# Layer 0's owners loaded by fours and its shared expert in batches; layer 3's split with merged stores and its first heads filled on two queues

## The chip, the cores and the metric

The kernel runs on one core of a Trainium2 chip. The core has five engines with instruction streams of their own, which wait for each other on semaphores: TensorE (PE in the rows; PEld is its loading of weights, PEq its sequencer), VectorE (DVE), ScalarE (ACT), GpSimd (POOL) and SyncE (SP), which here only starts DMAs. GpSimd starts DMAs too, above all gathers and scatters by an index. The metric is the device time of one execution in microseconds; the time before is the median of three runs.

## What is computed

A decoder of four layers works on 2,048 tokens of 256 numbers (in this kernel 16 tiles of 128 tokens, or 4 groups of 512). Two of its parts are touched. The first is the feed-forward part of layer 0, a mixture of 32 experts of 128 inner columns, of which each token uses 8, and a shared expert that every token uses:

```python
def _L0_ffn_ref(hidden_states, Wr, br, Wg_s, bg_s, Wu_s, bu_s, Wd_s, bd_s, Wg, bg, Wu, bu, Wd, bd):
    aff = jax.nn.sigmoid(jnp.dot(x, Wr) + br)
    top_v, top_i = jax.lax.top_k(aff, K)                       # K = 8 of 32
    top_w = top_v / (jnp.sum(top_v, axis=-1, keepdims=True) + 1e-09)
    w_full = zeros.at[jnp.arange(T)[:, None], top_i].set(top_w)
    shared = jnp.dot(silu(jnp.dot(x, Wg_s) + bg_s) * (jnp.dot(x, Wu_s) + bu_s), Wd_s) + bd_s
    gate = silu(jnp.einsum('th,ehi->eti', x, Wg) + bg[:, None, :])
    up = jnp.einsum('th,ehi->eti', x, Wu) + bu[:, None, :]
    down = jnp.einsum('eti,eih->eth', gate * up, Wd) + bd[:, None, :]
    return shared + jnp.einsum('te,eth->th', w_full, down)
```

The second is the attention of layer 3, with 16 heads of 16 columns over all 2,048 tokens at once:

```python
def _L3_attn_ref(x, proj_w, proj_b, wq, wk):
    proj = jnp.einsum('bsd,ed->bse', x, proj_w) + proj_b
    flat = proj by heads: (H, B * S, hd)
    q = jnp.einsum('hnd,hde->hne', flat, wq)
    k = jnp.einsum('hnd,hde->hne', flat, wk)
    attn = jax.nn.softmax(jnp.einsum('hne,hme->hnm', q, k) / jnp.sqrt(D), axis=-1)
    out = jnp.einsum('hnm,hmd->hnd', attn, flat)
```

Both are called as `x = x + part(layernorm(x))`.

## The kernel before

**Layer 0's experts** (`l0_ffn`). Tokens are routed, and each token's row is scattered by GpSimd into tiles of 128 rows that belong to one expert each: 63 + 95 + 63 = 221 tile units. A table in memory, `owner`, holds the expert's number of each tile. TensorE's loop takes the units as a pipeline: in iteration u it transposes the tile of unit u+3 (`turn`, L2117), makes gate and up of unit u+2 (`up`: a bias product, L2127, and two products, L2133), the down product of unit u (`down`, L2149, behind a wait for VectorE's copy of the hidden rows), and the transposition of the hidden rows of unit u+1 (`turn_hidden`, a wait at L2139, the transposition at L2140). The weights of `up` and `down` are chosen by the expert's number, which must stand in a register of TensorE's sequencer. At the start of each 24th iteration a load (L2109) brings 24 of them. ScalarE copies the transposed tile and makes the silu; VectorE takes the result (`take`, L2340), copies the transposed hidden rows (L2349) and multiplies gate and up (L2355); in between it combines finished tokens at places that a table, COMBINED, fixes. SP reads tiles and writes results from a ring of four places.

Behind the tiles the same loop runs 16 more units for the shared expert, one for each tile of tokens: a bias product (L2130), two up products from the transposed tokens (L2133), the product with the chosen weights that brings the experts' down biases (L2147), the down product (L2149), the transposition (L2140), and an addition to x by VectorE (L2343). The tokens not yet combined are combined behind it.

**Layer 3's split** (`l3_attn`). For each of four groups of 512 tokens VectorE adds the gathered rows of layer 2's experts to x (L4567), takes mean and variance and normalises (L4549); TensorE transposes (L4508); ScalarE and VectorE copy one half each (L4594, L4554); TensorE projects (L4520) and makes queries and keys (L4530) by turns in two banks; ScalarE copies each with rounding to a shorter form (L4609, the first part) and VectorE subtracts that from it (L4561, the second part); SP stores both parts in device memory, eight stores of 256 KB a group (L4490). GpSimd gathers the rows (L4626) and then fills two lines of ones in each of four half tiles of keys (L4631).

**Layer 3's heads.** The heads go in eight pairs. For each pair SP loads three copies of 16 rows per head for queries and for keys from device memory (L4687), and two lines of zeros (L4689), 14 DMAs in all, the pairs by turns in two tiles. TensorE first makes the values (L4706), then probes (L4727), whose maxima VectorE takes (L4782), then scores and products with the values. The first probe waits for the 14 loads of pair 0.

The order on each engine is the order in which the code writes it; no planner stands in between. Instructions wait for semaphores alone.

Of the kernel before, what the change touches and what calls it, by code (L numbers as in the profile page):

```python
# [1847 lines left out]
def l0_ffn(k):  # L1848
# [16 lines left out]
    UNITS = BATCH + ALL  # L1865
    BATCHED = 24
# [3 lines left out]
    with ExitStack() as stack:  # L1870
# [3 lines left out]
        shared_bias = sb(k, stack, "shared_bias", [P, DIM])  # L1874
# [17 lines left out]
        affinity, rest = sb(k, stack, "affinity", [P, 8, E]), sb(k, stack, "rest", [P, 8, E])  # L1892
# [4 lines left out]
        mine, slots = sb(k, stack, "mine", [P, E * 8]), sb(k, stack, "slots", [P, E * 8])  # L1897
# [12 lines left out]
        tile_out = k.normed  # L1910
# [18 lines left out]
        def out_bank(u):  # L1929
            return k.ps[:, 5 + u % 2, 0:DIM]  # L1930

# [55 lines left out]
        with phase(k, "experts", names) as (block, s), ExitStack() as more:  # L1987
            for r in range(4):
                s[f"wrote{r}"] = more.enter_context(nc.semaphore(f"experts_wrote{r}"))
# [9 lines left out]
            def _(sp):  # L1999
# [6 lines left out]
                for m in range(ALL + 7):  # L2006
# [7 lines left out]
                    if m >= 7:  # L2014
                        j = m - 7
                        g = group_of(j)
                        sp.wait_ge(s["out_taken"], j + 1)
                        sp.dma_start(back_dram[g][sl(j - BEGIN[g]), :], tile_out[:, j % 4, :]).then_inc(s[f"wrote{j % 4}"], 16)
                for r in range(4):
                    sp.wait_ge(s[f"wrote{r}"], 16 * len(range(r, ALL, 4)))  # L2020

            @block.gpsimd
            def _(pool):
# [18 lines left out]
                for g in range(2):  # L2042
                    for r in range(4):
                        pool.wait_ge(s[f"wrote{r}"], 16 * len(range(r, BEGIN[g] + TILES[g], 4)))
# [9 lines left out]
            def _(pe):  # L2054
# [41 lines left out]
                def weight(u, at, width):  # L2096
                    if not is_tile(u):
                        return experts[:, E, at:at + width]
                    return experts[:, bass.ds(expert_of[u], 1), at:at + width].rearrange("p o d -> p (o d)")

                def turn(m):
                    if m == 0:
                        for job in (("choose", 2), ("own", 1)):
                            job_taken(pe, job)
                    if m % BATCHED == 0:
                        count = min(BATCHED, ALL - m)
                        if m <= BEGIN[2] < m + count:
                            job_taken(pe, ("own", 2))
                        _, values = nc.values_load_multi_w_load_instructions(  # L2109
                            owner[0:1, m:m + count], engines=[mybir.EngineType.PE], min_val=0, max_val=E - 1,  # L2110
                            skip_runtime_bounds_check_because="the owners are clamped to the last expert")
                        expert_of.update({m + j: value for j, value in enumerate(values)})
# [7 lines left out]
                def up(u):  # L2120
                    if u >= 2:
                        pe.wait_ge(s["multiplied"], u - 1)
                    t = u - ALL
                    if is_tile(u):
                        if u == 0:
                            pe.wait_ge(s["weighted"], 16 * 5)
                        nc.tensor.matmul(gate_bank(u), one_hot[:, u:u + 1].broadcast_to([3 * E, P]), bias_parts[:, :], start=True, stop=False)  # L2127
                        pe.wait_ge(s["tile_copied"], u + 1)
                    else:
                        nc.tensor.matmul(gate_bank(u), k.ident[:, 0:1].broadcast_to([P, P]), shared_bias[:, :], start=True, stop=False)  # L2130
                    for kt in range(KD):
                        x = tileT[:, u % 2, sl(kt)] if is_tile(u) else xT[t // GROUP][:, kt, sl(t % GROUP)]
                        last = nc.tensor.matmul(gate_bank(u), x, weight(u, 2 * kt * INNER, 2 * INNER), start=False, stop=kt == KD - 1)  # L2133
# [8 lines left out]
                def down(u):  # L2142
                    if u >= 2:
                        pe.wait_ge(s["out_taken"], u - 1)
                    if not is_tile(u):
                        t = u - ALL
# [3000 lines left out]
```

## Time and profile before

| | us |
|---|---|
| runs | 3310.62, 3321.85, 3310.62 |
| median | 3310.62 |
| the profiled execution's own time | 3318.16 |
| its span | 3315.8 |
| tile units of layer 0 (window) | 482 to 907 |
| additions of the shared expert | 909.2 to 941.5 |
| layer 3's split, first projection to first matmul of the heads | 2301.9 to 2362.3 |

Busy time over the whole span, from the page:

```profile
PE 2973.0 (90%) x20865; PEld 1843.2 (56%) x20865; DVE 2232.8 (67%) x4489; ACT 1809.1 (55%) x4182; POOL 1123.5 (34%) x1288
```

These shares are means over four layers with different limits, so the stretches that the diff touches have to be read one by one. Rows of the kinds below are read like this: a timeline row has its start, its length, engine, line, operation, output <- inputs and how many instructions it stands for, and in brackets how long the engine had been idle and what released it; a row by line has least, median and longest duration in ns. A matmul of 32-bit numbers stands as two records (two passes).

### The profile page before, as it was taken

To read this page: it belongs to the slowest core of one execution; us is meant where nothing else is said; L and a number is where in the kernel's file an instruction comes from. 1 tells how busy PE (TensorE), PEld (TensorE's weight loads), DVE (VectorE), ACT (ScalarE), POOL (GpSimd) and SP (SyncE) were. 2 spreads that over 40 slices of the span, in tenths; PEclk is the share of its full clock that TensorE was granted. 3 is DMA by queue.
4 is the path that set the end of the run, shared out by engine and by line. 5 is a ranking of instruction groups with operands and counts; after the bars stand their busy time and mean duration, and the time that the engine had idled before them with its cause. 6 is when DMAs were issued, how large, how long until landed. Compare 5 with 4: busy or idle time off the path is not lost. (4 is left out here: it accounts for less than half of the span.)

```text
span 3315.8 us, 59147 instructions
## 1 busy us (share of the span) xinstructions
PE 2973.0 (90%) x20865; PEld 1843.2 (56%) x20865; DVE 2232.8 (67%) x4489; ACT 1809.1 (55%) x4182; POOL 1123.5 (34%) x1288
## 2 busy tenths in 40 slices
PE   7979759999998799988799989787799999999989
PEld 4656548888755466643567757454333333333667
DVE  6777655455667566677577647424589999996772
ACT  6958723333333344445566645221278888888554
POOL 3535564442442022124266653012111112211333
PEclk9999859999999999999899999898889999999989
DMA  9400066666630000031000042132501111110400
GB/s 303 140 10 1 1 249 197 210 199 178 184 108 20 27 1 1 1 111 70 15 1 1 1 153 76 65 110 72 135 1 21 21 21 21 21 21 1 141 1 26
DMA packets 158226, 243.58 MB, mean 73 GB/s; under 512 B 21298, under 2 KB 130482, under 8 KB 152482
## 3 DMA queue, kind: packets, MB, share of 16 engines
q1 hardware_dynamic: 144114, 202.05, 19.9%
q0 software_dynamic: 13824, 37.77, 3.6%
q8 instruction: 172, 2.82, 0.4%
q14 instruction: 116, 0.95, 0.1%
HBM read 132.64 MB, written 107.10 MB: 72 GB/s over the span
## 5 line engine op out<-in xcount | busy, mean ns | idle before, releaser
L4782 DVE TENSOR_REDUCE peaks<-ps 128x2 f32<-128x1024 f32 x512 | 616.1, 1220 | 38.3 <-PE ps L4727 32.0
L4821 ACT ACTIVATE attn<-ps 128x512 f32<-128x512 f32 x1024 | 556.0, 596 | 97.3 <-PE ps L4717 38.5
L4727 PE MATMUL ps<-keys,queries 50*128 50x512 f32 x1024 | 375.2, 463 | 12.6 <-DVE peaks L4782 8.0
L4717 PE MATMUL ps<-queries,keys 50*128 50x512 f32 x1024 | 377.6, 454 | 0.0
L4741 PE MATMUL ps<-attn,head_values 128*32 128x256 f32 x4096 | 330.8, 395 | 2.5 <-ACT output L4832 0.4
L4717 PEld LDWEIGHTS ps<-queries,keys 50*128 50x128 f32 x1024 | 154.9, 188 | 206.5 <-ACT attn L4821 195.0
L1239 POOL TENSOR_TENSOR attn_w<-attn_w,attn_share 128x512 f32<-128x512 f32 x128 | 131.7, 1050 | 372.0 <-DVE attn_share L1085 372.0
L2133 PE MATMUL ps<-experts,tileT 128*128 x884 | 229.7, 382 | 0.0
L2340 DVE COPY normed<-ps 128x256 f32<-128x256 f32 x221 | 93.8, 424 | 183.5 <-PE ps L2149 181.7
L4741 PEld LDWEIGHTS ps<-attn,head_values 128*32 128x32 f32 x4096 | 82.2, 108 | 190.5 <-ACT attn L4821 171.5
L2194 ACT ACTIVATE tileT<-ps 128x256 f32<-128x256 f32 x221 | 84.8, 384 | 149.5 <-PE ps L2117 149.5
L4727 PEld LDWEIGHTS ps<-keys,queries 50*128 50x128 f32 x1024 | 149.8, 191 | 23.3 <-DVE peaks L4782 16.6
L2133 PEld LDWEIGHTS ps<-experts,tileT 128*128 128x128 f32 x884 | 151.8, 192 | 15.7 <-issue 0.5
L2200 ACT ACTIVATE gate<-ps 128x128 f32<-128x128 f32 x237 | 65.8, 278 | 163.7 <-PE ps L2133 163.7
L1076 DVE TENSOR_REDUCE attn_peak<-ps 128x4 f32<-128x512 f32 x128 | 87.6, 685 | 94.8 <-PE ps L958 94.8
L2149 PE MATMUL ps<-experts,hiddenT 128*128 (+1 forms) x474 | 144.9, 387 | 7.3 <-DVE hiddenT L2349 5.5
L4871 POOL CAST peak_parts<-peak 128x8 fp32r<-128x8 f32 x32 | 6.3, 198 | 393.9 <-DVE peak L4788 377.4
L2050 POOL DMA_INDIRECT rows<-expert_rows,index x96 | 91.5, 954 | 127.0 <-DMA expert_rows<-normed 60.8
L972 PE MATMUL ps<-xT,L_xattn_Wq 128*128 128x512 f32 x256 | 125.7, 614 | 7.7 <-ACT qT L1176 6.2
L2038 POOL DMA_INDIRECT routed_rows<-rows,index x96 | 95.6, 996 | 83.8 <-DVE normed L2340 58.4
L4886 POOL CAST queries<-peak_rows 2x128 fp32r<-2x128 f32 x256 | 73.5, 287 | 126.5 <-DVE peak_rows L4794 113.0
L2117 PE MATMUL ps<-ident,tile_in 128*128 128x128 f32 x442 | 85.6, 276 | 31.3 <-DMA tile_in<-routed_rows 20.4
(732 smaller groups left out, 7124.2 us busy)
## 6 DMA issues: line engine op xcount, KB each, us to landing
tile_in<-routed_rows SPq DMA_DIRECT2D x244, 128.0 KB, 2.3
expert_rows<-normed SPq DMA_DIRECT2D x221, 128.0 KB
routed_rows<-zeros SPq DMA_DIRECT2D x2, 8064.0 KB, 47.7
experts<-in_L_ffn_experts SPq DMA_DIRECT2D x4, 3072.0 KB, 21.0
routed_rows<-zeros SPq DMA_DIRECT2D x1, 12160.0 KB, 65.7
kT<-L_xattn_keys SPq DMA_DIRECT2D x8, 1024.0 KB, 4.8
v<-L_xattn_values SPq DMA_DIRECT2D x8, 1024.0 KB, 8.0
experts<-in_L_ffn_experts SPq DMA_DIRECT2D x8, 1024.0 KB
```

What stands on the lines that cost most here:

```text
L972: last = nc.tensor.matmul(query_bank, wq[:, kt, sl(4 * p + jj)], xT[g % 2][:, kt, :], start=kt == 0, stop=kt == KD - 1)
L1239: nc.gpsimd.tensor_tensor(w, w, share[:, n % 2, side, :].unsqueeze(2).broadcast_to([P, 4, P]), ALU.mult).then_inc(s_["scaled"], 1)
L2038: nc.gpsimd.indirect_dma_start(rows_dram[g][:, :], bass.IndirectOffsetOnAxis(index_of(slice(t, t + 1))[:, 0, c:c + 1], 0), rows[:, t, :], ...
L2050: nc.gpsimd.indirect_dma_start(rows[:, TOP * (t % 2) + c, :], None, back_dram[g][:, :], bass.IndirectOffsetOnAxis(index[:, t, c:c + 1], 0) ...
L2133: last = nc.tensor.matmul(gate_bank(u), x, weight(u, 2 * kt * INNER, 2 * INNER), start=False, stop=kt == KD - 1)
L2149: nc.tensor.matmul(out_bank(u), hiddenT[:, u % 2, :], weight(u, 2 * KD * INNER, DIM), start=is_tile(u), stop=True).then_inc(s["downed"], 1)
L2340: v.tensor_copy(tile_out[:, u % 4, :], out_bank(u)).then_inc(s["out_taken"], 1)
L4717: nc.tensor.matmul(bank(("score", n)), keys[pair % 2][rows, sl(kt)], queries[pair % 2][rows, sl(c, CHUNK)], start=True, stop=True).then_in ...
L4727: last = nc.tensor.matmul(k.ps[:, SB + p % PB, :], queries[pair % 2][rows, sl(t)], keys[pair % 2][rows, sl(c, CHUNK)], start=True, stop=True)
L4741: last = nc.tensor.matmul(mixed_bank[sl(strip, PAD), :], head_values[:, u // CHUNKS % 2, a, block, :], attn[:, (4 * m + 2 * half + a) % RI ...
L4782: v.tensor_reduce(peaks[:, r % 2, i // CHUNKS, :, i % CHUNKS], k.ps[:, at:at + 2, :], AX.X, ALU.max).then_inc(s["maxed"], 1)
L4821: nc.scalar.activation(attn[:, n % RING, :], bank(("score", n)), ACT.Exp, scale=1.0 / 16.0).then_inc(s["read"], 1)
```

## The change

It has two halves.

In layer 0, the owners are loaded by fours: `owners(m)` stands between the down product and the next hidden transposition, one iteration ahead of the unit that needs it. From unit 64 on, results go to eight places instead of four (the other four in a tile that is free by then), with eight semaphores. The shared expert leaves the loop: four batches of 512 tokens, with gate and up computed transposed (`shared_up`, four products of 512 columns), the biases as operands of the silu and of VectorE's product, so that neither a bias product nor a transposition is needed, then 16 down products with the product for the biases ahead of each; the first batch's up products are issued two units before the end of the tiles.

In layer 3's split, the two parts are stored by four stores of 512 KB a group; the first pair's queries and keys are copied from `parts` straight into their tiles, the queries by SP (six copies a group), the keys by GpSimd's queue (six a group), the lines of zeros by SP, the lines of ones by ScalarE. ScalarE makes both copies of the transposed tokens. Queries and keys have four banks. VectorE measures and normalises two groups ahead. The heads load from pair 1 on, and the first probe waits for no load.

The core of the diff (waits and names that follow from it are left out):

```diff
-    BATCHED = 24
+    LOADED = 4
+    WIDE = 64
...
+        def tile_out(u):
+            return outs[:, sl(u % 4, DIM)] if u >= WIDE and u % 8 >= 4 else k.normed[:, u % 4, :]
+
+        def out_before(u):
+            return u - 8 if u >= WIDE + 8 else u - 4 if u < WIDE + 4 else -1
...
+                def owners(m):
+                    count = min(LOADED, ALL - m)
+                    if m <= BEGIN[2] < m + count:
+                        job_taken(pe, ("own", 2))
+                    _, values = nc.values_load_multi_w_load_instructions(
+                        owner[0:1, m:m + count], engines=[mybir.EngineType.PE], min_val=0, max_val=E - 1,
+                        skip_runtime_bounds_check_because="the owners are clamped to the last expert")
+                    expert_of.update({m + j: value for j, value in enumerate(values)})
                 def turn(m):
-                    if m % BATCHED == 0:
-                        count = min(BATCHED, ALL - m)
...
+                def shared_up(i):
+                    if i == 1:
+                        pe.wait_ge(s["multiplied"], ALL)
+                    if i >= 2:
+                        pe.wait_ge(s["shared_multiplied"], i - 1)
+                    for half in range(2):
+                        for kt in range(KD):
+                            last = nc.tensor.matmul(shared_bank(i, half), experts[:, E, sl(2 * kt + half)], xT[i][:, kt, :], start=kt == 0, stop=kt == KD - 1)
+                    last.then_inc(s["shared_upped"], 1)
+
+                def shared_down(t):
+                    pe.wait_ge(s["out_taken"], ALL + t - 1)
+                    out = out_bank(ALL + t)
+                    nc.tensor.matmul(out, chosenT[t // GROUP][:, sl(t % GROUP)], bd[:, :], start=True, stop=False)
+                    pe.wait_ge(s["shared_multiplied"], t // GROUP + 1)
+                    nc.tensor.matmul(out, shared_hiddenT[t // GROUP % 2][:, sl(t % GROUP)], experts[:, E, 2 * KD * INNER:COLS],
+                                     start=False, stop=True).then_inc(s["downed"], 1)
...
+                    if u == ALL - 2:
+                        shared_up(0)
                     if u >= 0:
                         down(u)
-                    if 0 <= u + 1 < UNITS:
+                    if is_tile(u + 4) and (u + 4) % LOADED == 0:
+                        owners(u + 4)
+                    if is_tile(u + 1):
                         turn_hidden(u + 1)
+                for i in range(GROUPS):
+                    if i + 1 < GROUPS:
+                        shared_up(i + 1)
+                    for t in range(GROUP * i, GROUP * i + GROUP):
+                        shared_down(t)
...
+                def shared_silu(i):
...
+                    nc.scalar.activation(shared_gate[i % 2], shared_bank(i, 0), ACT.Silu, bias=shared_bias[:, 0:1]).then_inc(s["shared_silued"], 1)
...
+                def shared_multiply(i):
...
+                    v.scalar_tensor_tensor(shared_hiddenT[i % 2], shared_bank(i, 1), shared_bias[:, 1:2], shared_gate[i % 2],
+                                           ALU.add, ALU.mult).then_inc(s["shared_multiplied"], 1)
...
+                def first_pair(engine, g, side, part, done):
+                    dst, order = ((queries[0], Q_PARTS), (keys[0], K_PARTS))[side]
+                    for place in (at for at, kind in zip(PLACES, order) if kind == part):
+                        for a in range(2):
+                            to = TILE * a + place
+                            engine.dma_start(dst[to:to + D, sl(g, GT)].bitcast(F32), parts[g % 2][sl(a, D), part, side * KD, :].bitcast(F32)).then_inc(done, 16)
...
-                        for part, ready in enumerate((s["first"], s["second"])):
-                            for i in range(2 * KD):
-                                sp.wait_ge(ready, 2 * KD * g + i + 1)
...
+                        for side in range(2):
+                            for part, ready in enumerate((s["first"], s["second"])):
+                                sp.wait_ge(ready, 2 * KD * g + KD * side + 1)
+                                if side == 0:
+                                    first_pair(sp, g, side, part, s[f"stored{g % 2}"])
+                                sp.wait_ge(ready, 2 * KD * g + KD * side + KD)
+                                row0 = (side * 2 + part) * DIM
+                                sp.dma_start(parts_dram[row0:row0 + DIM, sl(g, GT)].rearrange("(m p) n -> p m n", p=P),
+                                             parts[g % 2][:, part, sl(side, KD), :].bitcast(F32)).then_inc(s[f"stored{g % 2}"], 16)
...
-                            nc.tensor.matmul(k.ps[:, 6 + i % 2, :], w[:, m, :], flat[g % 2][:, m, :], start=True, stop=True).then_inc(s["qk_made"], 1)
+                            nc.tensor.matmul(k.ps[:, 4 + i, :], w[:, m, :], flat[g % 2][:, m, :], start=True, stop=True).then_inc(s["qk_made"], 1)
...
+                    for g in range(2):
+                        measure(g)
+                        normalise(g)
                     for g in range(GROUPS):
...
+                        if g + 2 < GROUPS:
+                            measure(g + 2)
                         for i in range(2 * KD):
                             subtract(g, i)
+                        if g + 2 < GROUPS:
+                            normalise(g + 2)
...
-                    for i in range(2):
-                        for side in range(2):
-                            row0 = TILE * side + 2 * D
-                            nc.gpsimd.memset(keys[i][row0:row0 + 2, :].bitcast(F32), 1.0).then_inc(s["lined"], 1)
...
+                    for g in range(GROUPS):
+                        for part, ready in enumerate((s["first"], s["second"])):
+                            pool.wait_ge(ready, 2 * KD * g + KD + 1)
+                            first_pair(pool, g, 1, part, s[f"kept{g % 2}"])
...
-                for pair in range(PAIRS):
+                for pair in range(1, PAIRS):
...
-                        pe.wait_ge(loaded[pair % 2], 16 * 14 * (pair // 2 + 1))
+                        if pair:
+                            pe.wait_ge(loaded[pair % 2], loads_of(pair))
```

**TensorE, in a tile unit whose successor opens a new load.** First the order before (`owner` is the table of experts' numbers, L2149 the down product, L2140 the hidden transposition, L2117 the tile's transposition, L2127 the bias product):

```order
L2133 MATMUL ps<-experts,tileT 128x256
L2133 ISA
L2133 MATMUL ps<-experts,tileT 128x256
L2149 ISA
L2149 MATMUL ps<-experts,hiddenT 128x256
L2140 MATMUL ps<-ident,hidden 128x128
L2109 TENSOR_LOAD owner
L2117 MATMUL ps<-ident,tile_in 128x128 x2
L2127 MATMUL ps<-bias_parts,one_hot 128x256
```

The order of the changed kernel at such a place (its lines are L2157 down, L2121 load, L2151 hidden transposition, L2133 tile's transposition, L2141 bias, L2144 up):

```order
L2144 MATMUL ps<-experts,tileT 128x256
L2144 ISA
L2144 MATMUL ps<-experts,tileT 128x256
L2157 ISA
L2157 MATMUL ps<-experts,hiddenT 128x256
L2121 TENSOR_LOAD owner
L2151 MATMUL ps<-ident,hidden 128x128
L2133 MATMUL ps<-ident,tile_in 128x128 x2
L2141 MATMUL ps<-bias_parts,one_hot 128x256
```

The load moved ahead of the hidden transposition, and it stands in every fourth unit instead of every 24th.

**SP, storing two groups of layer 3's split.** Before, where L4490 is a store of one of the four tiles of a part, and L4687 the first load of the heads:

```order
L4484 DMA zero_rows<-zeros 16x256
L4490 DMA parts<-parts_332 128x512 x8
L4490 DMA parts<-parts_333 128x512 x8
L4490 DMA parts<-parts_332 128x512 x8
L4490 DMA parts<-parts_333 128x512 x8
```

In the changed kernel (L4545 a copy into the first pair's queries, L4569 a store of two tiles):

```order
L4557 DMA zero_rows<-zeros 16x256
L4560 DMA queries_321<-zero_rows 2x2048 x2
L4545 DMA queries_321<-parts_330 16x512 x4
L4569 DMA parts<-parts_330 128x2x512
L4545 DMA queries_321<-parts_330 16x512 x2
L4569 DMA parts<-parts_330 128x2x512 x3
L4545 DMA queries_321<-parts_331 16x512 x4
L4569 DMA parts<-parts_331 128x2x512
```

Eight stores of a group became four, with six copies of 16 rows among them.

**GpSimd, behind the sixteen gathers of the split.** Before, with the lines of ones of both tiles of keys:

```order
L4626 DMA expert_rows<-back_rows,place_back 128x256 x16
L4631 MEMSET keys_325 2x2048 x2
L4631 MEMSET keys_326 2x2048 x2
```

In the changed kernel, with the key copies of the first pair (`parts_330` and `parts_331` are the split's two turns):

```order
L4545 DMA keys_323<-parts_330 16x512 x6
L4545 DMA keys_323<-parts_331 16x512 x6
L4545 DMA keys_323<-parts_330 16x512 x6
L4545 DMA keys_323<-parts_331 16x512 x6
```

The fills are gone from this engine, and 24 copies stand there.

## Rows read from the trace of the kernel before

**Rows 1.** windows: busy us (and instructions) per engine, granted clock, DMA share, GB/s

```profile
482.00:907.00 425.00, 406.89 (x2268) 342.83 (x2269) 234.15 (x808) 152.25 (x451) 181.16 (x190) 0.99 0.64 196
844.00:847.00 3.00, 3.00 (x10) 2.35 (x9) 0.11 (x1) 0.66 (x2) 1.70 (x2) 0.50 0.53 163
2331.60:2344.60 13.00, 10.09 (x25) 3.87 (x24) 8.55 (x23) 4.58 (x9) 0.00 (x0) 0.89 0.44 161
2362.30:2377.80 15.50, 10.86 (x42) 8.90 (x42) 1.76 (x1) 2.99 (x5) 5.88 (x5) 0.83 0.99 134
2389.00:3030.00 641.00, 630.82 (x5875) 235.00 (x5877) 618.97 (x594) 542.71 (x1028) 119.52 (x407) 0.97 0.12 17
```

**Rows 2.** timeline of TensorE in the tile units: start us, length us, [idle before <- releaser]

```profile
574.60 0.27 PE L2140 MATMUL ps<-ident,hidden 128*128 128x128 f32 x1
574.71 0.38 PE L2117 MATMUL ps<-ident,tile_in 128*128 128x128 f32 x2
575.90 0.59 PE L2149 MATMUL ps<-experts,hiddenT 128*128 x2
576.34 0.27 PE L2140 MATMUL ps<-ident,hidden 128*128 128x128 f32 x1
577.97 0.30 PE L2117 MATMUL ps<-ident,tile_in 128*128 128x128 f32 x1 [1.36 <-issue]
```

**Rows 3.** loads of owners and one wait, by line: ns min/median/max, first and last start

```profile
L2109 PEldq TENSOR_LOAD <-owner x10: 841/1944/2040, 462.6 to 890.7; - x10
L2109 PEldq TENSOR_LOAD <-owner x1: 1987/1987/1987, 575.8 to 575.8; - x1
L2109 PEldq TENSOR_LOAD <-owner x1: 841/841/841, 890.7 to 890.7; - x1
L2139 PEldq EVENT_SEMAPHORE  x1: 51/51/51, 575.7 to 575.7; - x1
```

**Rows 4.** waits of TensorE, 482 to 907 us: total us, times, longest us

```profile
PE ps L2117 <- issue: 10.9, 9, 1.6
PE ps L2149 <- DVE hiddenT L2349: 5.2, 15, 0.8
```

**Rows 5.** shared expert's additions, by line

```profile
L2343 DVE TENSOR_TENSOR x<-ps,x x16: 424/425/425, 909.2 to 941.5; 128x256 f32<-128x256 f32 x16
```

**Rows 6.** timeline of the split

```profile
2301.85 5.17 PE L4520 MATMUL ps<-xT,L_attn_proj_w 128*128 128x512 f32 x8 [0.83 <-ACT xT L4594]
2307.94 7.47 POOL L4631 MEMSET keys<- 2x2048 f32 x4
2356.76 0.69 DVE L4561 TENSOR_TENSOR parts<-ps,parts 128x512 fp32r<-128x512 f32 x1 [0.35 <-ACT parts L4609]
```

**Rows 7.** by line: normalisations and gathers of the split, scattering gathers of layer 0

```profile
L4549 DVE TENSOR_SCALAR normed<-x,moments,rstd x16: 396/411/2024, 2298.5 to 2341.5; 128x256 f32<-128x256 f32 x16
L4626 POOL DMA_INDIRECT expert_rows<-back_rows,place_back x16: 946/946/1213, 2287.7 to 2307.0; - x16
...
  issue: 4.6, 15
...
L2038 POOL DMA_INDIRECT routed_rows<-rows,index x96: 956/960/2788, 435.0 to 599.6; - x96
```

**Rows 8.** stores of the split in the DMA view, median us to landing last

```profile
parts<-parts SPq DMA_DIRECT2D x32, 256.0 KB, 2.5
```

**Rows 9.** timeline where the heads begin

```profile
2362.30 10.85 PE L4706 MATMUL ps<-L_attn_proj_w,xT 128*128 128x256 f32 x40 [6.21 <-PEq L61]
2362.36 1.25 SPq L4687 DMA_DIRECT2D queries<-parts  x3
2377.79 1.22 PE L4727 MATMUL ps<-keys,queries 50*128 50x512 f32 x4 [4.64 <-DMA queries<-zero_rows]
2378.94 3.78 PE L4706 MATMUL ps<-L_attn_proj_w,xT 128*128 128x256 f32 x8
2383.64 1.99 PE L4706 MATMUL ps<-L_attn_proj_w,xT 128*128 128x256 f32 x8
```

More of the change, by code:

```diff
@@ L1987, in l0_ffn @@
         with phase(k, "experts", names) as (block, s), ExitStack() as more:
-            for r in range(4):
+            for m in ("shared_upped", "shared_silued", "shared_multiplied"):
+                s[m] = more.enter_context(nc.semaphore(f"experts_{m}"))
+            for r in range(8):
                 s[f"wrote{r}"] = more.enter_context(nc.semaphore(f"experts_wrote{r}"))
@@ L2042, in _ @@
                 for g in range(2):
-                    for r in range(4):
-                        pool.wait_ge(s[f"wrote{r}"], 16 * len(range(r, BEGIN[g] + TILES[g], 4)))
+                    for u in range(BEGIN[g + 1] - 8, BEGIN[g + 1]):
+                        written(pool, u)
                     for t in range(FIRST[g], FIRST[g] + SIZES[g]):
@@ L2096, in weight @@
                 def weight(u, at, width):
-                    if not is_tile(u):
-                        return experts[:, E, at:at + width]
                     return experts[:, bass.ds(expert_of[u], 1), at:at + width].rearrange("p o d -> p (o d)")
+                def owners(m):
[6 more added lines that the diff above has]
+                    expert_of.update({m + j: value for j, value in enumerate(values)})
                 def turn(m):
                     if m == 0:
-                        for job in (("choose", 2), ("own", 1)):
-                            job_taken(pe, job)
-                    if m % BATCHED == 0:
-                        count = min(BATCHED, ALL - m)
[L2107 to L2112, printed above, removed]
+                        job_taken(pe, ("choose", 2))
                     pe.wait_ge(s[f"read{m % 4}"], 16 * (m // 4 + 1))
@@ L2208, in _ @@
                 act.wait_ge(s["outered"], 1)
-                for u in range(-3, UNITS):
+                for u in range(-3, ALL):
                     for job in LATE:
@@ L2397, in _ @@
                         combine(t, c)
+                shared_multiply(0)
+                shared_multiply(1)
+                for i in range(GROUPS):
+                    for t in range(GROUP * i, GROUP * i + GROUP):
+                        shared_take(t)
+                    if i + 2 < GROUPS:
+                        shared_multiply(i + 2)
                 for t in LEFT:
@@ L4615, in _ @@
                         if g + 1 < GROUPS:
-                            root(g + 1)
                             take_x(g + 1)
```

160 lines of the change are left out of this document (89 added, 71 removed).

## The prediction

> **What bounds the kernel now.** I read the page's slices first, then windows over the places that the diff touches, then the timeline inside them. In the tile units of layer 0 TensorE is the bound: 406.9 of 425 us busy at granted clock 0.99, VectorE 234 [rows 1]. The same group shows the other stretches: in one group of layer 3's split TensorE is busy 10.1 of 13.0 us and VectorE 8.6, the DMA share 0.44, so a chain between engines sets the pace; at the start of the heads the DMA share is 0.99; and behind 2389 us TensorE and VectorE are both 97% busy. So a gain in the units counts only as TensorE time, a gain in the split counts as the end of the phase, which waits for its last store, and what the heads start earlier they keep to the end.
>
> **Part 1, owners.** One unit takes 1.74 us (two hidden transpositions, 574.60 to 576.34) [rows 2]. A load of 24 owners begins at 575.8 and takes 1.99 us; the next matmul starts at 577.97, about 0.17 after the load ends. Without it the matmul would follow the transposition by 0.11, as it did at 574.71 [rows 2, 3]. Over the stretch such gaps are 10.9 us in 9 [rows 4]; with the 0.16 by which each gap's last transposition is drawn out over its 0.11, 12.3 us. All of this goes: **-12.3**. After the load at 841.6 the clock was also at 0.50 for 3.0 us [rows 1], so 1.5 us of work were lost: **-1.5**.
>
> Added: 55 loads inside the loop, of four values (one of one). No load of four is in the trace. Ten loads run from 0.84 to 2.04, and the 0.84 is the one of five values [rows 3]; 24 values cost 1.99, so each further value costs (1.99-0.84)/19 = 0.06, and four cost 0.78. The new place is between a unit's down product and the next hidden transposition. There TensorE's sequencer is ahead: the wait in front of the transposition was passed at 575.7, and the transposition began at 576.34, 0.64 later [rows 2, 3]. A load costs what it is longer than that lead, plus the 0.17 behind it: 0.78+0.17-0.64 = 0.31, times 55 = 16.8. Some fall into units in which TensorE already waits for VectorE's combining (5.2 us in 15 waits [rows 4]; by the kernel's table of combining there are twelve such places of four units, so one load in each at about 0.15): -1.8. So **+15.0**. Behind a waiting load stand only the transposition and the next unit's matmuls; VectorE's copy of the hidden rows waits for them, and it is not the bound. Bounds: if values come at one price per four, (1.99-0.84)/4 = 0.29 per four, a load of four is 0.55 and costs 0.08, in all 4 to 5; if four cost as much as five (0.84), 0.37 each or 20; and if no lead survives, 0.95 each or 52.
>
> The Trainium skill, page "DMA: Bandwidth & Descriptors", section "Latency and other measured facts", says that a tensor_load has a floor of about 600 ns and that loads are unrolled by four to spread it. The shortest load here, 841 ns with five values, lies above that floor; by it four values cost 0.13 us each behind the lead, an estimate, and the sum of this part would be some 8 us lower.
>
> Part 1 with eight result places: no wait of VectorE for the writing of a result is in the list of waits, so the places cost and give nothing. Sum **+1.2**.
>
> **Part 2, shared expert.** In the before, each of 16 units costs TensorE a bias product, two up products, a bias-of-down product and a down product, each of 256 columns at 0.43 (575.90 to 576.34), and a transposition of 0.11 [rows 2]: 2.26 us, 36.2 in all; its adds span 32.3 us, and the last two units lack the up work [rows 5]. After it: four batches of four products of 512 columns, twice 0.43 each = 13.6; 16 times two products of 256 columns = 13.7; together 27.3. The silu and the product of one batch, 512 columns on ScalarE and VectorE, stand behind the up products of the next; where they are not covered by eight products of 256 columns they show as a stall, at most the pair of them, about 1.4 (two operations of about 0.69, as the VectorE subtraction of 512 columns [rows 6]); I take 0.6 three times. 29.1 against 36.2: **-7.1** (-9 with no stall, -4.5 with full ones). Layer 0 in all: **-5.9**, from -20 to +2 (the loads at 20, the stalls full).
>
> **Part 3, layer 3's split.** Before: the first projection starts at 2301.85 and runs partly at half clock, 5.17 us [rows 6]. Then POOL fills four lines of keys from 2307.94 on for 7.47 us [rows 6], and the four normalising operations of the second group, elsewhere 0.41 each, take up to 2.02 [rows 7]; the second transposition waits for them. That cost 7.70 instead of 1.4 us. From then on one group follows another by 13 us, since each of its four query and key products waits for a bank that VectorE frees. The last subtraction starts at 2356.76 [rows 6], a store lands 2.5 us after its issue [rows 8], and the next phase's first matmul is at 2362.30 [rows 9]. I put the end of the phase at 2361.8.
>
> After: the memset on POOL is gone, ScalarE writes the key lines; group 1 is normalised before group 0 is projected; the four products have four banks. Then TensorE alone sets the pace: per group 8 passes for the projection and 8 for queries and keys at 0.43, and 8 transpositions at 0.11: 7.7 us. The first projection starts 0.6 later, since ScalarE makes both copies: 2302.4 to 2307.4; queries and keys of group 0 end at 2311.7; the last group's at about 2334.5; the last subtraction 1.4 later.
>
> Two queues carry more. SP issues 10 DMAs a group instead of 8; at 0.42 (three in 1.25 [rows 9]) they take 4.2 of the 7.7, and the last store goes out near 2339 and has landed by 2341.5. POOL issues six key copies a group. No direct copy from POOL to a tile is in the trace; the nearest is the gather of 128 rows, sixteen of them at 0.95 and 0.31 between (4.6 us in 15) [rows 7], so six are 7.5 us. They start when a group's keys are split, so the last six are over at 2342.1; the last is issued at 2340.8 and lands, like a store, 2.5 later: 2343.3. That ends last: **-18.5**. Bounds: below by SP's price of an issue, with the end set by the last group's splitting, near 2339 and -22.8; above by the longest gather, 2.79 [rows 7], which is rival (d). Transfers: stores of 2 MB took 0.44 of 13.0 = 5.7 us of all 16 engines [rows 1]; a group's 12 copies of 16 rows, 0.39 MB, put up to 2.9 more into it, at the pace of the loads of the pair, 134 GB/s at share 0.99 [rows 1]: rival (b).
>
> The SP wait in front of the query copies holds back the stores behind it, and those only; POOL has nothing else in this phase but the 16 gathers, which are out before.
>
> **Part 4, start of the heads.** Before, the value products run from 2362.30 for 10.85 us, and the first probe starts at 2377.79 after 4.64 us of waiting for the first pair's loads [rows 9]: **-4.6**, since the pair is already there. Eight value products then took 3.78 at half clock, against 1.99 a little later [rows 9]; without the pause TensorE stays at its full clock: 1.8, and 0.4 on the probes: **-2.2** (nothing, if the 9 us of waiting at the end of the phase cost the clock instead). Layer 3 in all: -18.5-4.6-2.2 = **-25.3** (-20 to -30).
>
> **Sum.** -5.9-25.3 = -31.2 on the profiled execution's 3318.2 gives 3287.0. That execution lies 7.5 above the median of the runs shown, 3310.6, so the forecast is **3279.5**.
>
> **Rivals.** (a) Short loads at their floor: a load of four at 0.57 costs 0.10, 55 of them 5.5 instead of 16.8: 11 to 12 less, **3268**. For it: 0.84 for five values is one row, and nothing shows the slope between five and 24; against: the load of 0.84 was followed by a gap as long as its excess over its lead.
> (b) The split is bound by transfers: 5.7+2.9 = 8.6 a group from 2312 on, end 2346.5 instead of 2343.3: **3283**. For: share 0.99 where copies of 16 rows ran; against: only 0.44 for the stores.
> (c) The loads find no lead, since a stall of one unit leaves the sequencer without one at the next: 0.95 each, 52 instead of 16.8, less 2 or 3 in the waits that are there: **3312**. For: TensorE's queue runs dry at each load; against: the lead is set by VectorE's copy, and three units without a load lie between.
> (d) Slower: the POOL queue becomes the bound of the split. VectorE's operations that have both operands in the on-chip memory (combining, normalising) and POOL hold each other up: with the memset beside them, one normalisation took 2.02 instead of 0.41 [rows 7]. If each of the 24 copies takes 2.79+0.30 (the longest gather [rows 7]), they end at 2311.7+24*3.09 = 2385.9, landed at 2387.5, 25.7 later than before: +25.7-6.8-5.9 = +13, **3324**. It decides from 2.55 us a copy on, where the total is nought. Against: 96 gathers beside the tile units have a median of 0.96 [rows 7], the 16 in this phase run at 0.95 while VectorE combines [rows 7], and VectorE has some 3 us of such work in 7.7 (four combining and four normalising operations).
> The Trainium skill, page "SBUF — State Buffer", section "A bandwidth-pool intuition that's wrong (but worth ruling out)", states this rule: a DMA issued from GpSimd of about 620 ns alone takes about 3100 ns beside a VectorE copy, as its descriptors can't be written meanwhile. The sixteen gathers at 0.95, with VectorE's combining beside them, don't show it, so it keeps a small chance.
>
> **How the numbers follow.** Forecast 0.56 (its own range 3271 to 3290), (a) 0.14, (b) 0.15, (c) 0.08, (d) 0.07. A measurement can't tell less than about 0.5%, 16.5 us, from no change: faster means below 3294, slower above 3327. Forecast, (a) and (b) lie below 3294, less 0.07 for their upper tails: faster 0.78. (c), those tails and half of (d) lie between, 0.18; slower 0.04. Range **3262 to 3302**: (a) with the shared expert and the split at their better ends, up to (b) with the loads at 20 and the stalls full, and a part of (c).
>
> **What would show it.** The 57 owner loads: the short ones near 0.78, with gaps of about 0.15 to 0.3 before the hidden transposition; at 0.57 rival (a), and gaps near 0.9 rival (c). 16 shared adds at the end with no more than 29 us of TensorE's work. Normalisations of 1.4 us a group and a cadence of 7.7 in the split; POOL's copies at 0.95 and 0.3, or near 3 for (d); the heads' first matmul 18 us earlier, counted from the gathers; the first probe right behind the fifth pair of value products. The forecast is wrong if the split's cadence stays above 9, or if the tile units take longer than before by more than 5 us.

## The result, and the profile after

The changed kernel took 3258.9 us (median of 4 runs, 3256.3 to 3262.4) against 3310.6 before: ratio 0.985, interval 0.983 to 0.987. The forecast was 3279.5, with a range from 3262: right in sign, short by 21 us, and the time lies 3 us below the range. The profiled execution took 3259.7 us, its span 3257.9.

Where the time went can be read stage by stage, from the starts of a few instructions in the traces (second column of "changed": another execution of it, from the first experiment):

| stage, from and to | before | changed | forecast | measured |
|---|---|---|---|---|
| first to last result of the tile units | 418.2 | 404.9, 406.5 | +1.2 | -12 to -13 |
| from there to the end of the last shared addition | 35.0 | 25.8, 25.8 | -7.1 | -9.2 |
| split's first gather to the heads' first matmul | 74.6 | 60.5, 60.2 | -18.5 | -14.2 |
| from there to the ninth reduction of the heads | 28.8 | 21.4, 21.7 | -6.8 | -7.3 |
| sum | | | -31.2 | -42 to -44 |

The two profiled executions differ by 58, so 14 lie in stages that the change doesn't touch. Those vary by themselves: over 14 executions of kernels that are alike there, the start up to the first tile result took 482.7 to 490.8 us, and the middle stages, from the last shared addition to the split's gathers, 1332.7 to 1347.1. The times of the first experiment, with 11 runs of before, give 44 as well (3302.8 to 3259.0).

The first two rows need two corrections, both seen by comparing with the experiment "layer 3 alone" below, which has the tile units of before. First, the 418.2 holds slow spells of TensorE's clock that belong to this one execution: granted clock 0.91 over the first 20 us, and the 0.50 of [rows 1] behind the load at 841.6. Layer 3 alone has the same code there, a clock of 1.00, and took 414.6 (first row before, second row layer 3 alone):

```profile
488.70:508.70 20.00, 20.00 (x114) 17.22 (x113) 6.90 (x28) 9.09 (x21) 7.67 (x8) 0.91 0.45 149
484.30:504.30 20.00, 20.00 (x123) 17.53 (x122) 8.47 (x39) 9.63 (x23) 8.56 (x9) 1.00 0.50 166
```

Second, the changed kernel makes the first shared batch's up products (L2166) ahead of the last tile results, so some of the shared expert's work is counted in the first row:

```profile
881.96 3.60 PE L2166 MATMUL ps<-xT,experts 128*128 128x512 f32 x8
886.90 0.69 PE L2157 MATMUL ps<-experts,hiddenT 128*128 x2 [0.80 <-DVE hiddenT L2401]
```

Against layer 3 alone, both with the clock at 1.00 in the first 20 us, the changed kernel gains 11.5 us up to the third-last tile result and loses 1.9 over the last two. So the loads give about 11.5, and the shared expert 9.2-1.9 = 7.3.

The windows of the changed kernel (columns as in [rows 1]); they answer to the tile units, the split, and the start and rest of the heads:

```profile
476.00:887.00 411.00, 403.66 (x2261) 338.80 (x2262) 234.14 (x806) 152.04 (x450) 181.09 (x189) 1.00 0.65 202
2282.00:2314.00 32.00, 21.21 (x61) 9.76 (x59) 14.34 (x35) 17.15 (x25) 10.90 (x22) 0.88 0.91 297
2315.90:2326.60 10.70, 10.63 (x40) 8.91 (x40) 1.76 (x1) 2.39 (x4) 4.40 (x4) 0.82 0.97 129
2335.00:2970.00 635.00, 624.80 (x5845) 233.59 (x5843) 615.67 (x591) 539.75 (x1023) 119.49 (x407) 0.97 0.12 17
```

The second row is the new thing: over 32 us of the split the DMA share (the mean busy share of the 16 DMA engines) is 0.91, where one group of before had 0.44.

The owners' loads by line, the list of TensorE's waits over the tile units, and a stretch of its timeline, in the changed kernel (L2151 is the hidden transposition, L2157 the down product, L2133 the tile's transposition):

```profile
L2121 PEldq TENSOR_LOAD <-owner x56: 308/334/535, 456.5 to 876.8; - x56
```

```profile
PE ps L2133 <- DMA tile_in<-routed_rows: 18.0, 1, 18.0
PE ps L2157 <- DVE hiddenT L2401: 5.5, 15, 0.8
PE ps L2157 <- issue: 1.6, 10, 0.2
```

```profile
568.72 0.27 PE L2151 MATMUL ps<-ident,hidden 128*128 128x128 f32 x1
568.83 0.38 PE L2133 MATMUL ps<-ident,tile_in 128*128 128x128 f32 x2
569.05 0.28 PE L2141 MATMUL ps<-bias_parts,one_hot 96*128 96x256 bf16 x1
569.16 1.03 PE L2144 MATMUL ps<-experts,tileT 128*128 x4
570.03 0.59 PE L2157 MATMUL ps<-experts,hiddenT 128*128 x2
570.46 0.27 PE L2151 MATMUL ps<-ident,hidden 128*128 128x128 f32 x1
```

A load of four takes 0.334 us, not 0.78. The 10.9 us of gaps of [rows 4] have no successor in the list: no wait by "issue" stands in front of a transposition any more, while the waits for VectorE's copy stayed (5.2, now 5.5). The 18.0 is the wait for the first tile, ahead of the units. The shared expert's additions by line span 20.5 us instead of the 32.3 of [rows 5]:

```profile
L2395 DVE TENSOR_TENSOR x<-ps,x x16: 414/425/426, 892.5 to 913.0; 128x256 f32<-128x256 f32 x16
```

The split's timeline after (answers to [rows 6]): L4597 the projections, L4545 the copies of the first pair, L4569 the stores, L4633 the subtractions, the last one here:

```profile
2269.96 6.40 PE L4597 MATMUL ps<-xT,L_attn_proj_w 128*128 128x512 f32 x8 [1.17 <-ACT xT L4668]
2280.51 3.60 PE L4597 MATMUL ps<-xT,L_attn_proj_w 128*128 128x512 f32 x8
2280.74 3.28 POOL L4545 DMA_DIRECT2D keys<-parts  x6 [5.04 <-ACT parts L4682]
2288.25 3.60 PE L4597 MATMUL ps<-xT,L_attn_proj_w 128*128 128x512 f32 x8
2295.99 3.60 PE L4597 MATMUL ps<-xT,L_attn_proj_w 128*128 128x512 f32 x8
2303.51 4.15 SPq L4545 DMA_DIRECT2D queries<-parts  x4
2303.88 0.69 DVE L4633 TENSOR_TENSOR parts<-ps,parts 128x512 fp32r<-128x512 f32 x1 [0.17 <-ACT parts L4682]
2309.71 2.04 SPq L4569 DMA_DIRECT2D parts<-parts  x3
```

The groups follow each other by 7.74 (2280.51, 2288.25, 2295.99), as forecast. But the last subtraction ends at 2304.6 and the last store goes out only at 2311.7, behind query copies that take SP about 1 us each. The rows by line (answers to [rows 7]) and the DMA view, median us to landing last ([rows 8]):

```profile
L4626 DVE TENSOR_SCALAR normed<-x,moments,rstd x16: 395/406/499, 2266.3 to 2290.7; 128x256 f32<-128x256 f32 x16
```

```profile
L4545 SPq DMA_DIRECT2D queries<-parts x24: 507/736/1612, 2278.9 to 2308.9; - x24
L4545 POOL DMA_DIRECT2D keys<-parts x24: 484/486/808, 2280.7 to 2305.7; - x24
```

```profile
parts<-parts SPq DMA_DIRECT2D x16, 512.0 KB, 3.7
keys<-parts POOLq DMA_DIRECT2D x24, 32.0 KB, 3.0
```

Where the heads begin (answers to [rows 9]):

```profile
2315.97 10.76 PE L4796 MATMUL ps<-L_attn_proj_w,xT 128*128 128x256 f32 x40 [12.76 <-PEq L61]
2326.66 0.73 PE L4818 MATMUL ps<-keys,queries 50*128 50x512 f32 x4
2327.33 2.00 PE L4796 MATMUL ps<-L_attn_proj_w,xT 128*128 128x256 f32 x8
```

TensorE now waits 12.8 us for the end of the split instead of 6.2; the first probe follows the value products without a wait, and the next eight value products take 2.00 at a granted clock of 1.00; before they took 3.78 at 0.50.

### The profile page after: what moved, and what is told of

Same layout as the page of the kernel before. It is cut to its first block and busy times, and to the rows that moved or that the text cites. A ratio compares the mean times of both kernels' runs of the same rounds, so it can differ in the third digit from the quotient of the medians.

```text
span 3257.9 us, 58960 instructions
## 1 busy us (share of the span) xinstructions
PE 2934.4 (90%) x20781; PEld 1815.0 (56%) x20785; DVE 2219.2 (68%) x4457; ACT 1814.7 (56%) x4178; POOL 1127.2 (35%) x1308
## 5 line engine op out<-in xcount | busy, mean ns | idle before, releaser
L2144 PE MATMUL ps<-experts,tileT 128*128 x884 | 228.2, 380 | 0.0
L2144 PEld LDWEIGHTS ps<-experts,tileT 128*128 128x128 f32 x884 | 151.2, 191 | 15.2 <-issue 0.5
L2157 PE MATMUL ps<-experts,hiddenT 128*128 x442 | 134.5, 386 | 7.3 <-DVE hiddenT L2401 5.5
L2384 DVE COPY normed<-ps 128x256 f32<-128x256 f32 x144 | 61.1, 424 | 113.9 <-PE ps L2157 112.5
L4322 POOL TENSOR_TENSOR lasting<-lasting,pairs 128x512 f32<-128x512 f32 x64 | 80.9, 1278 | 86.2 <-ACT lasting L4247 86.2
```

The lines of the kernel that those rows point to most:

```text
L2144: last = nc.tensor.matmul(gate_bank(u), tileT[:, u % 2, sl(kt)], weight(u, 2 * kt * INNER, 2 * INNER), start=False, stop=kt == KD - 1)
L2157: nc.tensor.matmul(out_bank(u), hiddenT[:, u % 2, :], weight(u, 2 * KD * INNER, DIM), start=True, stop=True).then_inc(s["downed"], 1)
```

## The experiments

The theory after the result: (A) loads of four are short enough to vanish in the sequencer's lead; (b), from the prediction: transfers now bind the split's end. All stage lengths below are read as in the table above. The letters of the theories are those of the expectation that stands ahead of each result. The seven executions whose split is that of the changed kernel took 59.3 to 60.5 us there, so a difference of 1 us in the split is no effect. Only the first four experiments were timed in several rounds; the others are one execution each and are read by their traces.

**Which half gives what.** The changed kernel again; layer 0's edits alone; layer 3's edits alone.

> The changed kernel once more, as the common measure for its partial versions on one chip. Both theories: 45 to 52 us below the kernel before.

> Only layer 0's edits (owners by fours, eight places, shared batches); layer 3 as before. Theory A (the loads of four last 0.33 us, are wholly inside the sequencer's lead of 0.64, and cost nothing; all long gaps are gone): 13.8 for the loads and 9 for the shared expert, so 22 to 23 us below before. Theory B (the loads cost what was forecast, and the rest of the difference between the two traces lies in stages that nothing touches, above all a slower clock in the first 60 us of the trace of before): 6 to 8 us below before.

> Only layer 3's edits; layer 0 as before. Theory A: 22 to 26 us below before, as the traces differ from the gathers of the split to the first probes by 21 and over the heads by 3. Theory B (the 3 us inside the heads are the clock's and not the change's): 20 to 22.

Ratios to before, five rounds: the whole 0.986 (0.984 to 0.988), layer 0 alone 0.995 (0.993 to 0.997), so -17 us with -11 to -22, layer 3 alone 0.994 (0.991 to 0.996), so -20 with -13 to -28. The whole came out at -44, one short of the expected 45 to 52. Layer 0's traces decide better than its times: with its edits 35.0 became 25.8 in the shared expert, and the units took 406.3 instead of the 414.6 of layer 3 alone. That is 17.5, between the theories but far from B's 6 to 8. It is below the 22 to 23 of A mostly because A counted from the 418.2 of before, 3.6 more than layer 3 alone took for the same code, by its slow clock. For layer 3 the stages give 15.0 and 7.0, 22 in all, and the 3 us inside the heads are not the change's: from the ninth reduction to the last one layer 0 alone, whose heads are those of before, has 638.0 us and layer 3 alone 637.1, before 642.6, the changed kernel 639.9. So theory B of that run was right on this.

**The number of values in a load.**

```diff
-    LOADED = 4
+    LOADED = 24
```

> The changed kernel with 24 owners a load, at the changed place (behind the down product). Theory A (it is the number of values that matters): each of 9 loads inside the loop lasts 1.99 and shows a gap of 1.99+0.17-0.64 = 1.5 us, so 13 to 15 us slower than the changed kernel. Theory C (it is the place that matters: behind the down product the load lies beside TensorE's work): within 3 us of the changed kernel, gaps below 0.5.

Theory A came out: the units took 418.9 us, 12.4 more than the 406.5 of the changed kernel's second execution; 0.991 to before (0.990 to 0.994). The new place of the load gave nothing. The load and its gaps, by line and in the list of waits:

```profile
L2121 PEldq TENSOR_LOAD <-owner x10: 804/1930/2100, 455.5 to 884.7; - x10
```

```profile
PE ps L2151 <- issue: 11.0, 9, 1.5
```

With the 0.16 by which the down product before each gap is drawn out, 11.0 in 9 are the whole 12.4.

**What a load costs.** Different counts in one kernel:

```diff
-    LOADED = 4
+    COUNTS = (4, 1, 2, 3, 5, 6, 7, 8, 12, 16, 24)
```

> The changed kernel with loads of 4, 1, 2, 3, 5, 6, 7, 8, 12, 16 and 24 owners in turn, at the same place. Theory A1 (values come by fours, 0.33 us for each begun four): 1 to 4 values 0.33, 5 to 8 0.67, 12 1.0, 16 1.33, 24 2.0; gaps on TensorE from 8 values up, (length + 0.17 - 0.64). Theory A2 (a price per value, 0.083, from 4 at 0.334 and 24 at 1.99): 1 at 0.1, 5 at 0.42, 8 at 0.67, 12 at 1.0. Theory F (the forecast: 0.55 at the start and 0.06 a value, with the five of the kernel before at 0.84): 1 at 0.6, 5 at 0.84, 12 at 1.3.

None of the three theories fits: 1 value took 0.31, 2 took 0.54 to 0.78, 3 1.0, but 4 0.33, then 5 1.5 to 1.7, 6 1.7 to 2.0, 7 1.9 to 2.1, and again 8 0.75 to 0.83, 12 1.1, 16 1.3, 24 1.9 to 2.1. Since in this run all loads of 4, 8, 12, 16 and 24 began at an owner whose number is a multiple of four and 2, 3, 5, 6, 7 didn't, the next one mixed that too:

```diff
+    COUNTS = (4, 2, 4, 8, 2, 3, 4, 5, 6, 6, 7, 12, 1)
```

> The changed kernel with loads of 4, 2, 4, 8, 2, 3, 4, 5, 6, 6, 7, 12 and 1 owners in turn, so that fours and their multiples also begin at places of the table that are no multiple of four. Theory C (the count decides: multiples of four go by fours at about 0.33 and a bit, others one by one at about 0.3): 4 always 0.33, 8 0.8, 12 1.1; 2 0.6, 3 1.0, 6 1.8, 7 2.1 wherever they begin. Theory S (the start decides: from a multiple of four, fours are fetched at once and the rest one by one; from any other, all one by one): a four from such a start takes 1.2, an eight 2.4, a six from a multiple of four 0.33+0.6 = 0.9 and a seven 1.2.

Theory S came out. One row each, by line, in this order: 4 from a multiple of four; 4, 8 and 6 from two behind one; 6 from a multiple; 1.

```profile
L2126 PEldq TENSOR_LOAD <-owner x1: 348/348/348, 609.2 to 609.2; - x1
L2126 PEldq TENSOR_LOAD <-owner x1: 1172/1172/1172, 620.1 to 620.1; - x1
L2126 PEldq TENSOR_LOAD <-owner x1: 2561/2561/2561, 627.8 to 627.8; - x1
L2126 PEldq TENSOR_LOAD <-owner x1: 1713/1713/1713, 682.5 to 682.5; - x1
L2126 PEldq TENSOR_LOAD <-owner x1: 1046/1046/1046, 671.3 to 671.3; - x1
L2126 PEldq TENSOR_LOAD <-owner x1: 307/307/307, 733.5 to 733.5; - x1
```

From a multiple of four, whole fours come at 0.29 to 0.41 each and what remains one by one at about 0.3; from any other start all come one by one, at 0.26 to 0.35 (in loads of two, up to 0.5). So the five of [rows 3] were one four and one single, 0.63 by these prices. It measured 0.84 there, 0.80 in the kernel with 24 a load and 0.65 in layer 3 alone:

```profile
L2109 PEldq TENSOR_LOAD <-owner x1: 646/646/646, 882.9 to 882.9; - x1
```

And 1.99 for 24 is six fours. The gaps follow the forecast's formula: behind the load of 2.56, TensorE's timeline has

```profile
630.56 0.30 PE L2156 MATMUL ps<-ident,hidden 128*128 128x128 f32 x1 [1.92 <-issue]
```

With the 0.16 by which the matmul before is drawn out that is 2.08, and 2.56+0.17-0.64 = 2.09.

**Eight places.** With `WIDE = 1024`, that is, four places throughout:

> The changed kernel with four places for results instead of eight from unit 64 on. Forecast: they cost and give nothing, so the units from 64 to 220 take 285.3 us as in the changed kernel, within 0.5. Rival: with the long gaps gone VectorE now comes to a place before it is written out, and the units get some us longer.

285.4 us from unit 64 to 220, as with eight. The eight give nothing here.

**What ends the split.** Query copies moved to GpSimd's queue:

```diff
-                                if side == 0:
-                                    first_pair(sp, g, side, part, s[f"stored{g % 2}"])
...
+                        for side in range(2):
...
+                                first_pair(pool, g, side, part, s[f"kept{g % 2}"])
```

> The changed kernel with the first pair's query copies on GpSimd's queue too (12 a group there, none on SP). Rival (b), transfers are the bound of the split's end: same bytes, so from the split's first gather to the heads' first matmul 60 us as in the changed kernel, within 1. Theory S (SP's issues are the bound: the last group's six query copies take it 5.5 us with its stores behind them): 4 to 5 us less, 55 to 56.

Neither theory: 63.2, 3 more. SP now had issued its last store 52.0 us after the first gather (2322.2) instead of 56.3, but it landed 6.4 us later; SP was through at 2328.7, 1.6 us earlier than in the changed kernel, counted from the first gather. So issuing earlier bought 1.6 of 4.3: mostly (b). Then all engines waited until 2333.2, because GpSimd's last instruction of the phase lasted this long (by line, in this kernel and in the changed one):

```profile
L61 POOLq DRAIN  x1: 5282/5282/5282, 2327.8 to 2327.8; - x1
```

```profile
L61 POOLq DRAIN  x1: 3322/3322/3322, 2309.5 to 2309.5; - x1
```

Before it was 1.36 us. The phase has 16, 40 and 64 DMAs from GpSimd in the three kernels, so 0.08 us of draining for each. That is a price of this phase only: two phases of the changed kernel further ahead, with 224 and 32 DMAs from GpSimd, end with drains of 10.0 and 3.86 us, 0.04 and 0.12 for each. In the changed kernel the split's drain is over at 2312.8, under SP's wait until 2315.5.

Without the copies, the heads loading pair 0 as before:

```diff
-                for pair in range(1, PAIRS):
+                for pair in range(PAIRS):
```

> The changed kernel without the copies of the first pair: the heads load pair 0 from device memory as before, and the first probe waits for it; merged stores, four banks and the order ahead stay. Rival (b), transfers: the split's end comes 4 to 6 us earlier (54 to 56 from the first gather to the heads' first matmul), and the heads' start is 7 longer (28.5 from first matmul to ninth reduction instead of 21.6). Theory P (the end is set by the chain on TensorE, VectorE and ScalarE, and the copies only follow): within 1 of 60, and 7 longer at the heads.

Rival (b) came out: 54.2, 6.0 less, at a DMA share of 0.68 in the window of the split, and 28.6 at the heads, 7.0 more; the wait for the loads is back (timeline):

```profile
2276.00:2311.00 35.00, 28.91 (x84) 13.64 (x82) 19.74 (x50) 21.50 (x34) 1.12 (x2) 0.94 0.68 249
```

```profile
2311.31 10.52 PE L4784 MATMUL ps<-L_attn_proj_w,xT 128*128 128x256 f32 x40 [6.41 <-PEq L61]
2327.03 1.22 PE L4805 MATMUL ps<-keys,queries 50*128 50x512 f32 x4 [5.21 <-DMA queries<-zero_rows]
```

The copies of the first pair give 7 where the heads begin and take 6 where the split ends. This run takes SP's issues of the copies away together with their bytes; the run before took the issues alone, and gained SP 1.6.

**What made the groups shorter.** Lines of ones filled by GpSimd again; VectorE's and ScalarE's order as before; two banks.

> The changed kernel with the lines of ones filled by GpSimd again, behind the gathers and ahead of its copies, instead of by ScalarE. Forecast's view (the fill and the normalisations beside it hold each other up): the normalisations of one group take up to 2 us each instead of 0.35 to 0.41, and the split gets 3 to 6 us longer. Rival (b): the transfers have slack for that at the start, since they begin late: GpSimd's copies of group 0 go out 3 us later, and the end moves by 0 to 2 us.

> The changed kernel with VectorE's and ScalarE's order in the split as in the kernel before: a group is measured and normalised just ahead of the subtractions of the group before it, not two groups ahead. Theory O (it is this order that made a group last 13 us): TensorE's groups follow each other by 10 to 13 us again, and the split (60.2 us from first gather to the heads' first matmul) gets 7 to 12 us longer. Rival (b), transfers: they take 8.3 us a group anyway, so with groups by up to 9 us it gets no more than 3 longer.

> The changed kernel with two banks for queries and keys instead of four; the order ahead stays. Theory K (the banks made the cadence): each of the four products waits again for VectorE, 1.2 us each instead of 0.86, groups by 9 to 10, split 3 to 6 us longer than 60.2. Theory O: the banks matter little, within 2 of 60.2.

With the fills back 61.6 us, 1.4 more: one normalisation took 1.77, and the key copies began behind the fills. That is rival (b)'s view. With the old order 69.3, 9.1 more, as theory O had it: TensorE waits for a group's normalisations again (L4586 the transposition; start, length, idle before):

```profile
2290.09 3.60 PE L4597 MATMUL ps<-xT,L_attn_proj_w 128*128 128x512 f32 x8
2296.20 1.66 PE L4586 MATMUL ps<-ident,normed 128*128 128x128 f32 x8 [2.51 <-DVE normed L4626]
2302.55 3.60 PE L4597 MATMUL ps<-xT,L_attn_proj_w 128*128 128x512 f32 x8
2313.34 3.60 PE L4597 MATMUL ps<-xT,L_attn_proj_w 128*128 128x512 f32 x8
```

Two banks: 61.8, 1.6 more, within theory O's 2, although the groups now follow by 8.7 to 9.1, which is nearer theory K's cadence. Both 61.6 and 61.8 lie about 1 us above the spread of the unchanged split, each in one execution. So measuring two groups ahead is most of the split's gain, and fills and banks count little. That they count little because the copies and stores take nearly as long as a group is an argument; no run took fills or banks back without the copies.

## Why the prediction was wrong, step by step

- **Long loads, -12.3 and the clock, -1.5.** The gaps were read rightly: they are gone, with 24 a load they return as 11.0 us in 9, and their end is worth about 11.5. The clock's 1.5 was no term of the change: layer 3 alone and the kernel with 24 a load have long loads too, and no such spell.
- **55 short loads, +15.0.** This is the step that failed. It put a load of four at 0.78 by a line through 24 values (1.99) and five (0.84). But the price doesn't grow with the count alone: four aligned values cost 0.33, what one costs, and the five carried a single one at the full price. With 0.33+0.17 below the lead of 0.64, the whole term is nought. The lower bound, a price per four, was the right idea, spoilt by the intercept of the five, a single row that came out at 0.65 and 0.80 in other executions. Rival (a) went the right way and not far enough: no row gives its 0.57, and there is no floor near it, since loads of one value took 0.3.
- **Eight places, nothing.** Right.
- **Shared expert, -7.1.** About -7.3, once the first batch's up products are counted here, so right in size. The way was another: between the batches the three stalls of 0.6 aren't there (inside three of the batches TensorE waits 0.17 for an addition), and the longest wait, 0.80, is that of the last tile's down product, with no further tile to cover it.
- **Split, -18.5.** The cadence of 7.7 was right, the end was not: -14.2. GpSimd's copies were cheaper than the gathers (0.49 without a pause against 0.95 and 0.31), so its queue ended early, and rival (b) held: the DMA share was 0.91, and SP's own copies slowed from 0.51 at best to 1 us each. Rival (b)'s price, 3 us, was near the 4 that it took. Rival (d) didn't happen: beside VectorE's normalising and combining a copy took 0.60 to 0.81 instead of 0.48, far from the 2.55 at which (d) begins to decide.
- **Heads, -6.8.** -7.3, right with its parts: no wait, and full clock. But what the copies cost the split belonged in the same account: 6 of these 7 are paid there.

With the loads at nought and the other terms left, the sum would have been -46 (-45 without the clock's 1.5). Measured are -42 to -44 in the stages of the table, or -40 by the halves (17.5 and 22), which leave out the slow spells of before.

That the time came out below the range, and not just inside its lower end, is chance: the few runs of the result differ by 51.7 in their medians, the 11 and 5 of the first experiment by 43.8, and 43.8 below 3310.6 is 3266.8. That the forecast was short of those 43.8 by some 12 us is not chance: 15.0 of the short loads, less the 4 that the split gave too little.

Two small readings of the prediction were off and bear on nothing: the owner loads are 56, not 57, and behind 2389 us TensorE is 98% busy (630.8 of 641), not 97%.

## What to carry to other kernels

A price per piece from two different counts is no slope before one knows what a piece is; when a term is repeated 55 times, give its lower bound the same weight as the interpolation. Load registers from tables by aligned fours. A spell of the clock that one execution shows is not a term until a second execution shows it. Data copied ahead into a phase whose transfers are already dense only moves the wait: count its bytes against the phase that issues it.

## What the runs showed of the hardware

Register loads on TensorE's queue: aligned fours at about 0.33 us, single values at about 0.3, an unaligned twelve 3.1 to 3.5. GpSimd's drain at the end of the split: 1.36, 3.32 and 5.28 us with 16, 40 and 64 DMAs issued from it, and it can be what the phase ends with. A direct copy of 16 rows issued from GpSimd takes 0.48 us of its time, and 0.60 to 0.81 beside VectorE's normalising and combining. The Trainium skill, page "SBUF — State Buffer", section "A bandwidth-pool intuition that's wrong (but worth ruling out)", gives about 3100 ns for a DMA from GpSimd overlapped with a VectorE copy. The changed split has no VectorE copy, so no run here shows that case; beside the operations that it has, no copy took over 0.81 us. Filling two rows of 2,048 numbers takes GpSimd or ScalarE about 1.9.
